# A recurrent layer with fp16 pairs on one core: four element-wise steps of VectorE in full width where they stood in halves

## What is computed

```python
comb = jnp.concatenate([x_t, h], axis=-1)
z = jax.nn.sigmoid(comb @ Wz + bz)
r = jax.nn.sigmoid(comb @ Wr + br)
comb2 = jnp.concatenate([x_t, r * h], axis=-1)
h_cand = jnp.tanh(comb2 @ Wh + bh)
h_new = (1.0 - z) * h + z * h_cand
h_next = jnp.where(prop, jnp.tanh(h_new @ Wp + bp), h_new)
```

## Time and profile before

| | |
|---|---|
| time, median of 3 runs | 1055.98 us (1055.78 to 1056.47) |
| time of the profiled execution | 1056.31 us |
| its span, first to last instruction | 1054.5 us |
| mean granted TensorE clock | 0.999 |
| busy | PE 99%, PEld 92%, DVE 76%, ACT 65% |

### The profile page before, as it was taken

The page is one execution under the profiler, slowest core; times in us unless marked ns, Lnnn a source line. Parts: engine busy times, 40 slices in busy tenths (PEclk is TensorE's granted clock), DMA queues, the critical chain, the costliest instruction groups (busy, mean ns, idle before and its releaser), DMA issues.

```text
span 1054.5 us, 53898 instructions
## 1 busy us (share of the span) xinstructions
PE 1044.9 (99%) x23984; PEld 966.2 (92%) x23984; DVE 799.2 (76%) x2692; ACT 689.4 (65%) x1666; POOL 0.2 (0%) x4
## 2 busy tenths in 40 slices
PE   9999999999999999999999999999999999999997
PEld 3477999999999999999999999999999999999997
DVE  6989988877777777777777777777777776666665
ACT  4766767666666666666666666666675666565664
POOL 0000000000000000000000000000000000000000
PEclk9999999999999999999999999999999999999999
DMA  9312211101111001111001110011110000000001
GB/s 325 110 43 83 77 59 43 44 3 44 43 43 44 23 23 44 43 43 43 21 26 43 44 43 22 24 43 43 43 43 23 24 23 24 23 24 23 24 4 43
DMA packets 38344, 47.63 MB, mean 45 GB/s; under 512 B 2144, under 2 KB 33760, under 8 KB 37728
## 3 DMA queue, kind: packets, MB, share of 16 engines
q1 hardware_dynamic: 38112, 44.19, 12.4%
HBM read 27.40 MB, written 16.78 MB: 42 GB/s over the span
## 4 chain that ended last, share of the span: by engine, by line
PE 94%; DVE 4%; ACT 1%; DMA 1%; issue 1%; SPq 0%; DVEq 0%
PE acc L1122 54%; PE x_acc L1047 34%; PE x_acc L953 5%; PE x_acc L1072 1%; DVE mag L628 1%; DMA x_blk<-x_dram 1%; DVE wrec_lo L692 1%; DVE mag_x L631 0%; DVE win_lo L684 0%; ACT gate L504 0%; DVE x_lo L699 0%; ACT wrec_hi L498 0%; DVE x_lo L706 0%; DVE keep L883 0%; DVE x_blk L909 0%
## 5 line engine op out<-in xcount | busy, mean ns | idle before, releaser
L504 ACT ACTIVATE gate<-acc,unscale 128x128 f32<-128x128 f32 x702 | 239.0, 384 | 268.7 <-PE acc L1122 268.4
L1122 PE MATMUL acc<-h_split,wrec_hi 128*128 128x64 f16 x8192 | 343.8, 193 | 0.0
L1047 PE MATMUL x_acc<-x_hi,win_hi 128*128 128x256 f16 x1092 | 297.7, 273 | 0.0
L1047 PE MATMUL x_acc<-x_hi,win_lo 128*128 128x256 f16 x1092 | 297.6, 273 | 0.0
L1047 PE MATMUL x_acc<-x_lo,win_hi 128*128 128x256 f16 x1092 | 297.6, 273 | 0.0
L1122 PEld LDWEIGHTS acc<-h_split,wrec_hi 128*128 128x128 f16 x8192 | 283.1, 98 | 0.0
L1122 PE MATMUL acc<-q_split,wrec_hi 128*128 128x64 f16 x5088 | 215.5, 193 | 0.0
L1122 PE MATMUL acc<-h_split,wrec_lo 128*128 128x64 f16 x4096 | 203.2, 193 | 1.4 <-DVE h_split L898 1.4
L470 ACT ACTIVATE x_part<-x_acc,bias,part_unscale 128x256 f32<-128x256 f32 x312 | 159.0, 561 | 47.5 <-PE x_acc L1047 47.4
L1122 PEld LDWEIGHTS acc<-q_split,wrec_hi 128*128 128x128 f16 x5088 | 179.2, 98 | 0.0
L524 ACT ACTIVATE acc<-x_part,seed_scale 128x256 f32<-128x256 f32 x384 | 172.7, 477 | 0.1
(11 more groups left out here) (116 smaller groups left out, 1059.8 us busy)
## 6 DMA issues: line engine op xcount, KB each, us to landing
out_dram<-x_blk SPq DMA_DIRECT2D x30, 512.0 KB, 3.2
x_blk<-x_dram SPq DMA_DIRECT2D x24, 512.0 KB, 4.2
x_blk<-x_dram SPq DMA_DIRECT2D x3, 1024.0 KB, 8.8
x_blk<-x_dram SPq DMA_DIRECT2D x4, 256.0 KB, 4.0
x_part<-wz_dram SPq DMA_DIRECT2D x4, 256.0 KB, 7.0
x_part<-wh_dram SPq DMA_DIRECT2D x4, 256.0 KB, 6.6
x_part<-wr_dram SPq DMA_DIRECT2D x1, 1024.0 KB, 11.1
x_part<-wz_dram SPq DMA_DIRECT2D x1, 1024.0 KB, 13.3
```

The lines of the kernel that those rows point to most:

```text
L504: nc.scalar.activation(gate[g][:, half, :], acc[g][:, half, :], func, scale=unscale[:, g:g + 1]).then_inc(gate_ready[g], 1)
L1047: mm = nc.tensor.matmul(in_halves(x_acc[bank][:])[:, j], weights[g][:, slot_w, k, j * P:(j + 1) * P], in_halves(values[m % 2][:, slot_x, : ...
L1122: mm = nc.tensor.matmul(acc[g][:, j, :], weights[g][:, k, j * P:(j + 1) * P], values[:, k, lo, :], start=False, stop=False, skip_group_che ...
```

## The change

VectorE's program is changed in four places, and one wait of TensorE goes. `q_full`, the low part of `q_split` and h_out (with its semaphore counted in ones) are written by one 256-element instruction each, where two of 128 elements stood. The low part of `h_split` is written in full too, other than on the steps with a propagation, where the low part stays in halves. The hi parts stay in halves everywhere, but both halves of `new` are waited for ahead of the first of them.

```diff
-                for half in HALVES:
-                    nc.vector.tensor_tensor(q_full[:, half, :], gate[R][:, half, :], h_in[:, half, :], ALU.mult).then_inc(q_full_ready, 1)
-                for n, half in enumerate(HALVES):
-                    dve.wait_ge(q_hi_ready, 2 * t + n + 1)
-                    dve.wait_ge(q_full_ready, 2 * t + n + 1)
-                    subtract_hi(q_full, q_split, half).then_inc(q_lo_ready, 1)
+                nc.vector.tensor_tensor(q_full[:], gate[R][:], h_in[:], ALU.mult).then_inc(q_full_ready, 1)
+                dve.wait_ge(q_hi_ready, 2 * t + 2)
+                dve.wait_ge(q_full_ready, t + 1)
+                subtract_hi(q_full, q_split, slice(0, KC)).then_inc(q_lo_ready, 1)
...
+                dve.wait_ge(new_ready, 2 * t + 2)
                 if t + 1 < T:
-                    for n, half in enumerate(HALVES):
-                        dve.wait_ge(new_ready, 2 * t + n + 1)
+                    for half in HALVES:
                         nc.vector.tensor_tensor(split[:, half, 0, :], new[:, half, :], keep[:, half, :], ALU.subtract).then_inc(hi, 1)
-                for n, half in enumerate(HALVES):
-                    dve.wait_ge(new_ready, 2 * t + n + 1)
-                    nc.vector.tensor_tensor(h_out[:, half, :], new[:, half, :], keep[:, half, :], ALU.subtract).then_inc(h_new_ready, 1)
-                if t + 1 < T:
+                nc.vector.tensor_tensor(h_out[:], new[:], keep[:], ALU.subtract).then_inc(h_new_ready, 1)
+                dve.wait_ge(h_new_ready, t + 1)
+                if prop:
                     for n, half in enumerate(HALVES):
                         dve.wait_ge(hi, count + n + 1)
-                        dve.wait_ge(h_new_ready, 2 * t + n + 1)
                         subtract_hi(h_out, split, half).then_inc(lo, 1)
-                else:
-                    dve.wait_ge(h_new_ready, 2 * t + 2)
+                elif t + 1 < T:
+                    dve.wait_ge(hi, count + 2)
+                    subtract_hi(h_out, split, slice(0, KC)).then_inc(lo, 2)
...
-                pe.wait_ge(q_lo_ready, 2 * t + 1)
+                pe.wait_ge(q_lo_ready, t + 1)
                 rec(C, wrec_hi, q_split, LOW, 1)
-                pe.wait_ge(q_lo_ready, 2 * t + 2)
                 rec(C, wrec_hi, q_split, HIGH, 1).then_inc(product_done[C], 1)
```

## The result

The change makes the kernel slower: 1059.64 us (median of 8 runs, 1058.85 to 1060.16) against 1056.42 for the kernel before beside it (8 runs, 1055.78 to 1057.03), a ratio of 1.0028 with the 95% interval [1.002, 1.0037]. That is 3.2 us, with 2.1 to 3.9 as its bounds. The profiled execution took 1058.85 us (span 1056.8, granted clock 1.0), 2.5 more than that of before; it is the fastest of the eight.

The account below looks back on a forecast made before the run. The prediction took TensorE's matmul stream as the bound, VectorE's lateness costing only where PE waits. Its terms summed to 2.0 us on a median of 1055.98, giving 1058.0 us, range 1056.6 to 1061.0.

Parts of the forecast that it names:

- the mechanism: Whole kernel: VectorE's later results delay PE where it already waits, 1.4 to 2.8 us slower; chance 0.60.
- a late `q_split`: Rival: the low part reaches C too late in every step, 1 to 4 us or 6.4 us; chance 0.18.
- steps 1 and 2: VectorE is late already at these early steps, so each adds 0.21 us: 0.42 us.
- propagation of step 3, propagation of step 7: PE is waiting for the hi part there, which comes later: 0.17 us.
- steps 5 to 7, up to C of 7: VectorE has no idle time there, so the steps' debts add up: 0.71 us.
- steps 8 to 10: Forecast for steps 8 and 9 only: 0.25 us owed, 0.12 us idle, so 0.12 us.
- step 15: VectorE comes later to the x products; half taken, since an earlier pause need not fall there again: 0.12 us.
- steps 115 and 123: Late propagation steps, given no cost in the sum.
- ahead of the last step, and the end: PE gets `h_split` 0.17 us later and full h_out costs 0.11 us behind the last `new`: 0.28 us.
- The cheap separate wait: Rival: a separate wait costs no more than a carried one, 0.04 us; 0.9 us slower, 1056.9; chance 0.13.
- The faster case: Rival: operations occupy VectorE fully, so merges free 0.45 us a step, at most 1.2 us gained, 1054.8; chance 0.04.

Follow-up runs that it names:

- four_more: The changed kernel with four more one-column memsets at VectorE's start: 1058.81 us, ratio 1.0025 to the kernel before.
- q_only_ones: The kernel before with only the r times h part merged in every step, merged instructions counting ones on their semaphores: 1056.39 us, ratio 1.0.
- late_only_ones: The kernel before with all merges in steps 16 to 127 only, merged instructions counting ones on their semaphores: 1057.07 us, ratio 1.0007.
- q_only: The kernel before with only the r times h part merged in every step, merged instructions adding two to their semaphores: 1058.33 us, ratio 1.002.
- late_only: The kernel before with all merges in steps 16 to 127 only, merged instructions adding two to their semaphores: 1058.88 us, ratio 1.0025.
- both_in_one: The changed kernel with only the semaphore of q_split's low part counted in twos, both its waits in one separate instruction: 1061.43 us, ratio 1.0048 to the kernel before.
- early_only: The kernel before with all merges in steps 0 to 15 only, merged instructions adding two to their semaphores: 1059.05 us, ratio 1.0025.
- carried: The changed kernel with VectorE's waits reordered so the instruction carries the one that comes last: 1057.36 us, ratio 1.001 to the kernel before.

## Why the prediction came out as it did

The direction, the mechanism and the place were right: 0.28% slower, by results of VectorE that come later in the first steps and at the end, for the price of waits right behind the instruction waited for. 1059.64 lies inside the range to 1061.0, but 1.6 above the 1058.0. Of that 0.4 is the kernel before, which stood at 1056.42 beside it and at 1055.98 in the three runs of the forecast, and 0.6 is the trace's 2.57 against the sum of 2.0. The remaining 0.6 us lie within the interval of the difference; whether they are scatter or something that the one profiled execution lacks stays open. By the trace, 2.57 us, the mechanism is inside its 1.4 to 2.8, but the time is outside the 1057.4 to 1058.8 that the forecast gave as its own range. The room above that was kept for a late `q_split`, which did not happen, so that the time stayed within the whole range is in part luck.

The sum, term by term, from the shifts of the matmuls (what is left out is -0.1 together, in single pieces of under 0.03):

| term | forecast | after |
|---|---|---|
| steps 1 and 2 | 0.42 | 0.47 |
| propagation of step 3 | 0.17 | 0.56 |
| steps 5 to 7, up to C of 7 | 0.71 | 0.77 |
| propagation of step 7 | 0.17 | 0.20 |
| steps 8 to 10 | 0.12 | 0.24 |
| step 15 | 0.12 | 0.06 |
| step 72 | 0 | -0.06 |
| steps 115 and 123 | 0 | 0.14 |
| ahead of the last step, and the end | 0.28 | 0.28 |

Step 8 was to begin 1.6 us later and begins 1.98 later; the prediction's own terms up to there make 1.47.

The step that failed is the one on step 3. "PE is waiting, so each costs 0.17" was right for the wait, 0.20 in four_more and in step 7, but took it that VectorE's pauses stay where they stood. Removing 480 instructions moves every multiple of 64, and one of them fell on the only hi part of step 3 that PE waits for: 0.37. I treated the pause of step 15 as chance (half of it in the sum). It was a place in the program too, and the change did move it away; step 72's went as well, for a gain of 0.06.

The terms of steps 1, 2 and 5 to 7 were under-sized by a tenth or so: the separate wait measures 0.10, not 0.09, and the debt of a step 0.24, not 0.21. Steps 8 to 10 came to 0.24 for 0.12: 0.12 until step 9 begins, 0.06 more at its C, where the debt outlived the idle time, and 0.05 in the middle of C's low part of step 9, where no matmul waits for VectorE; q_only_ones has that gap too and four_more has not, and its cause is open. In steps 115 and 123, costed at nothing, the hi part of the propagation is late as in steps 3 and 7, which the list of PE's waits of before did not show as waits; late_only_ones has the same.

The low part of `q_split`, costed at nothing, did cost nothing: q_only_ones and the flat middle of the kernel after show it. Its cover was thinner than the 0.05 of the prediction, though. In step 44 the full low part is ready 0.95 behind the start of `q_full`, 0.27 later than the first half was, not 0.24, and 0.06 ahead of its reader, which by step 72 of before can start 0.05 behind the end. The rival with it, at 0.18, was nearer than the chance says, for 0.03 us more was enough, and four kernels of this study fell into it (q_only, late_only, both_in_one and, in its 16 steps, early_only). The cheap separate wait falls by the gaps (0.10 against 0.03) and by `carried`. The faster case falls with them: the two hi parts of step 44 and what follows them start 0.42 apart in all (406.44 to 406.86), 0.21 for an operation of 0.284, and the kernel with 480 instructions fewer is not the quicker one. (Its 0.45 counted three merges, where an ordinary step has four; its bound of 1.2 us does not depend on that.)

The Trainium skill (VectorE: DVE Perf Modes, "The DRAIN you can't avoid") says of eight copies in a row that a semaphore behind each of them adds nothing. It says nothing of where the wait stands, and `carried` against the kernel after shows that this matters: 0.03 behind the end with the wait carried, 0.10 with it apart, for the same two operations. The prediction also read it too narrowly. The same section adds that a next operation that is not held starts earlier, so the 0.08 by which independent operations overlap here is no disagreement with it.

## What to carry to other kernels

Merging two halves saved nothing here in the engine's busy time (798.7 us for 799.2), since the halves overlapped and the merged one has a reader that must wait for its end, and it lengthened the way from the first input to the first output. Count the latter wherever another engine stands waiting, and nothing where it doesn't. Where an instruction has several waits, let it carry the one that comes last (here the one written first), and leave the one that is met long before to the separate wait instruction: reordering three lines on TensorE gave 1.5 us, which is more than any merge here did. And a cover of a few 0.01 us is to be tested by the smallest change that could use it up (here a count of two), since in a loop of 128 steps it decides.

## What the runs showed of the hardware

- A wait that the instruction carries lets VectorE start 0.03 us behind the end of what it waits for, a separate wait instruction 0.10. A wait instruction with two waits gives 0.13 where the wait met last stands first in it (`q_full` in q_only and both_in_one) and 0.09 where it stands second (h_out and the low part of `h_split`, 406.86 to 407.36 in step 44 of the kernel after, the same in all 96 such steps). On TensorE a carried wait gives 0.06, a separate one 0.15.
- No instruction of VectorE that adds two to a semaphore carries a wait in the built programs, 60 to 420 of them in the kernels that have any.
- VectorE pauses for up to 0.37 us at some odd multiples of 64 of its instructions, and adding four of them early moved such a pause. The Trainium skill (Runtime: NRT & Kernel Launch, "Instruction fetch mechanics") says that instructions are refilled in blocks of 256 and that crossing from one to the next is mostly hidden. The traces here have pauses at counts that do not lie multiples of 256 apart (192 and 1856 in the kernel after are six and a half blocks apart), so either the block or the cause is another; no run here tells which.
